# State-space inputs: three chunks' step-size products move into the pipeline, with their copy on VectorE and the softplus at the end

## The reference

```python
xz = x @ in_proj_w.T
u, z = split(xz)                                   # 256 channels each
u = silu(causal_dwconv(u, conv_w, conv_b))         # 4 taps
x_dbl = u @ x_proj_w.T                             # 8 + 16 + 16 columns
dt, Bm, Cm = x_dbl[:8], x_dbl[8:24], x_dbl[24:]
delta = softplus(dt @ dt_proj_w.T + dt_proj_b)
y = selective_scan(u, delta, -exp(A_log), Bm, Cm) + u * D
y = y * silu(z)
return y @ out_proj_w.T
```

## Time and profile before

| what | value |
|---|---|
| runs | 2076.75, 2073.79, 2072.45 us (median 2073.79) |
| the profiled execution, its own time | 2079.87 us |
| its span in the trace | 2077.9 us |
| `mamba_inputs` of the first block | up to 62.64 us, where the scan's first instruction stands |
| `mamba_inputs` of the second block | 1192.11 to 1244.05 us |
| scans (64 scan instructions each) | 65.5 to 269.8 us and 1247.3 to 1451.4 us |
| mean granted clock of TensorE | 0.937 |

### The profile page before, as it was taken

The page is one execution under the profiler, slowest core; times in us unless marked ns, Lnnn a source line. Parts: engine busy times, 40 slices in busy tenths (PEclk is TensorE's granted clock), DMA queues, the critical chain, the costliest instruction groups (busy, mean ns, idle before and its releaser), DMA issues. The chain is left out here.

```text
span 2077.9 us, 46457 instructions
## 1 busy us (share of the span) xinstructions
PE 1798.5 (87%) x18012; PEld 902.7 (43%) x18012; DVE 1619.0 (78%) x3425; ACT 1117.0 (54%) x2083; POOL 542.9 (26%) x560
## 2 busy tenths in 40 slices
PE   6777788999799999997899977777768999999967
PEld 2222254444255555553444422222533555555534
DVE  5899965666788999984565559999658999998665
ACT  5544423222278888885322274443342888888815
POOL 2798930000200000001000029989230000000012
PEclk9899998999689999998799979999886999999969
DMA  5333300311312222211041004443012222222200
GB/s 174 117 122 120 123 11 0 82 51 31 102 30 49 53 53 57 53 27 26 3 87 51 26 20 133 124 121 102 1 43 77 49 54 57 56 61 44 34 8 21
DMA packets 64617, 127.37 MB, mean 61 GB/s; under 512 B 15959, under 2 KB 26741, under 8 KB 62925
## 3 DMA queue, kind: packets, MB, share of 16 engines
q1 hardware_dynamic: 64108, 123.88, 23.3%
q10 hardware_dynamic: 288, 0.52, 0.1%
HBM read 105.74 MB, written 17.43 MB: 59 GB/s over the span
## 5 line engine op out<-in xcount | busy, mean ns | idle before, releaser
L1644 ACT ACTIVATE a_probs<-a_ps_k 128x512 f32<-128x512 f32 (+3 forms) x1280 | 598.9, 545 | 229.6 <-PE a_ps_k L1556 129.8
L1538 PE MATMUL a_ps_q<-a_k_op,a_q_op 84*32 84x512 bf16 (+7 forms) x5120 | 536.5, 366 | 29.0 <-DVE a_maxes L1701 18.8
L1704 DVE TENSOR_REDUCE a_maxes<-a_ps_q 128x1 f32<-128x512 f32 x768 | 504.1, 686 | 65.9 <-PE a_ps_q L1538 63.2
L1552 PE MATMUL a_ps_k<-a_q_op,a_k_op 87*32 87x512 bf16 (+7 forms) x5120 | 518.9, 354 | 6.2 <-DMA a_q_op<-a_max_T 2.9
L1574 PE MATMUL a_ps_o<-a_probs,a_vh 128*32 128x512 f32 (+3 forms) x2752 | 318.7, 508 | 0.8 <-ACT a_probs L1644 0.8
L1538 PEld LDWEIGHTS a_ps_q<-a_k_op,a_q_op 72*32 72x32 bf16 (+1 forms) x5120 | 187.4, 97 | 175.2 <-DVE a_maxes L1704 68.7
L1701 DVE CUSTOM_DVE_ANT_0 a_ps_q<-a_ps_q,all_c_mask_q 128x128 f32<-128x128 f32 (+3 forms) x512 | 248.0, 496 | 7.6 <-PE a_ps_q L1538 6.4
L1552 PEld LDWEIGHTS a_ps_k<-a_q_op,a_k_op 75*32 75x32 bf16 (+1 forms) x5120 | 185.7, 96 | 141.7 <-ACT a_probs L1644 84.0
L979 ACT ACTIVATE e_silu<-e_psg,all_me_b 128x512 f32<-128x512 f32 x128 | 87.8, 687 | 227.9 <-PE e_psg L911 227.9
L1784 POOL CAST a_max_parts<-a_neg_max 128x16 bf16<-128x16 f32 x32 | 6.3, 197 | 756.1 <-DVE a_neg_max L1709 756.1
L1062 DVE SCALAR_TENSOR_TENSOR e_mid<-e_psv,all_me_b,e_silu 128x512 f32<-128x512 f32 x128 | 95.7, 749 | 129.3 <-PE e_psv L913 125.4
(11 more groups left out here) (265 smaller groups left out, 2396.9 us busy)
## 6 DMA issues: line engine op xcount, KB each, us to landing
m0sc_c_rows<-m_bc_rows SPq DMA_DIRECT2D x32, 512.0 KB, 3.6
e_w_rows<-e_comb SPq DMA_DIRECT2D x64, 256.0 KB, 3.2
m1sc_c_rows<-m_bc_rows SPq DMA_DIRECT2D x32, 512.0 KB, 3.6
a_outputs<-a_o_sb SPq DMA_DIRECT2D x512, 18.0 KB
a_q_op<-a_q_parts SPq DMA_DIRECT2D x30, 288.0 KB
a_k_op<-a_k_parts SPq DMA_DIRECT2D x30, 288.0 KB
m0sc_b_rows<-m_bc_rows SPq DMA_DIRECT2D x32, 256.0 KB
m1sc_b_rows<-m_bc_rows SPq DMA_DIRECT2D x32, 256.0 KB
```

The costliest lines, as they stand in the source:

```text
L1538: last = pe.matmul(ps_q[32 * r:32 * r + 32, use % QB, 0:width], q_op[h % SLOT][0:NR, part(t, r)], k_op[h % SLOT][0:NR, kc * CH:kc * CH + w ...
L1552: last = pe.matmul(ps_k[32 * r:32 * r + 32, b % KB, 0:width], k_op[h % SLOT][:, part(j, r)], q_op[h % SLOT][:, c * CH + first:c * CH + fir ...
L1644: act.activation(probs[:, n % PSLOT, 0:width], ps_k[:, b % KB, 0:width], ACT.Exp).then_inc(exp_done, 1)
L1704: dve.tensor_reduce(found, bank, AX.X, ALU.max).then_inc(q_read, 1)
```

## The change

The step-size products of chunks 0, 1 and 2 now follow the gate products of steps 2, 3 and 4; that of chunk 3 follows xd of chunk 3, as the last. VectorE copies those of chunks 0, 1 and 2 out of PSUM to `delta`, adding the bias, at the end of steps 2, 3 and 4, after the taps. ScalarE no longer has a softplus in the step loop. After the loop it takes the softplus of chunk 0 from SBUF in place (one instruction of 128x1024), the second part of chunk 3, the softplus of chunk 3 out of PSUM (two instructions, as before), and that of chunks 1 and 2 from SBUF. VectorE's last products are in the order 0, 3, 1, 2.

```diff
@@ mamba_inputs @@
+        dt_copied = m.sem("dt_copied")
@@ order of the products @@
-        for s in range(NC + 1):
+        for s in range(NC + 2):
             items += [("u", s, h) for h in range(NH2) if s < NC]
             items += [("xd", s - 2, 0)] if s >= 2 else []
-            items += [("gate", s - 1, h) for h in range(NH2) if s >= 1]
-        items += [("dt", c, h) for c in range(2) for h in range(NH2)]
-        items += [("xd", NC - 1, 0)]
-        items += [("dt", c, h) for c in range(2, NC) for h in range(NH2)]
-        reader = {"u": raw_copied, "xd": xd_ready, "dt": delta_ready, "gate": gate_ready}
+            items += [("gate", s - 1, h) for h in range(NH2) if 1 <= s <= NC]
+            items += [("dt", s - 2, h) for h in range(NH2) if s >= 2]
+        reader = {"u": raw_copied, "xd": xd_ready, "dt": dt_copied, "gate": gate_ready}
@@ ScalarE @@
             def softplus(c):
-                for h in range(NH2):
-                    act.wait_ge(made, product_made("dt", c, h))
-                    act.activation(delta[:, h, chunk(c)], bank("dt", c, h), ACT.Softplus,
-                                   bias=w["dt_b"][:, h:h + 1]).then_inc(delta_ready, 1)
+                act.wait_ge(dt_copied, NH2 * (c + 1))
+                act.activation(delta[:, :, chunk(c)], delta[:, :, chunk(c)], ACT.Softplus).then_inc(delta_ready, 1)
+
+            def last_softplus(h):
+                act.wait_ge(made, product_made("dt", NC - 1, h))
+                act.activation(delta[:, h, chunk(NC - 1)], bank("dt", NC - 1, h), ACT.Softplus,
+                               bias=w["dt_b"][:, h:h + 1]).then_inc(delta_ready, 1)
@@ ScalarE, step loop and tail @@
-                if s == NC + 1:
-                    softplus(0)
...
-            softplus(1)
+            softplus(0)
             second(NC - 1)
-            softplus(2)
-            softplus(3)
+            for h in range(NH2):
+                last_softplus(h)
+            for c in range(1, NC - 1):
+                softplus(c)
@@ VectorE, end of a step (after the taps) and tail @@
-            for c in range(NC):
-                dve.wait_ge(delta_ready, NH2 * (c + 1))
+                if 2 <= s <= NC:
+                    for h in range(NH2):
+                        dve.wait_ge(made, product_made("dt", s - 2, h))
+                        dve.tensor_scalar(delta[:, h, chunk(s - 2)], bank("dt", s - 2, h), w["dt_b"][:, h:h + 1], None,
+                                          ALU.add).then_inc(dt_copied, 1)
+            for n, c in ((1, 0), (3, NC - 1), (4, 1), (5, 2)):
+                dve.wait_ge(delta_ready, n)
                 dve.tensor_tensor(du[:, :, chunk(c)], delta[:, :, chunk(c)], u[:, :, chunk(c)], ALU.mult).then_inc(du_ready, 1)
```

## The result

The changed kernel takes 2090.74 us (median of 4, 2090.15 to 2095.76), the kernel before beside it 2075.27 (4 runs, 2072.45 to 2077.39): ratio 1.0063, 95% interval 1.0039 to 1.0087, so 8 to 18 us slower. The forecast had the direction, and its 6.2 us are about half of the size; its range, up to 2084.5, does not hold the time.

A forecast was written before the change was run, and what follows sets the result against it. No engine bounds the whole; the chain through the two inputs sections to the scan counts. First block +1.9, second +1.2, together +3.1, plus clock +3.1, is +6.2 us: 2073.79 gives 2080.0, range 2075.0 to 2084.5.

The forecast's parts named there:

- Steps 1 to 5: Inputs section up to the last xd: VectorE waits for step-size products; X +0.8 us in the first block, +1.1 second.
- X: When ScalarE reads xd of chunk 3; first block 54.33 us before, 55.1 forecast at full clock.
- Step 6: Tail from X to the scan: table load and softplus follow X; +1.1 us in the first block, +0.1 in the second.
- Step 7: TensorE's clock may fall ahead of u of chunk 3 and the last xd, each block; 0.75 to 0.8 us each, +3.1.
- Full clock at all four places: Rival: TensorE keeps full clock ahead of u of chunk 3 and the last xd; +3.1 us, 2076.9; chance 0.20.
- The wait costs nearly nothing: Rival: VectorE's wait is nearly free, with short taps and brief copies; 0 to +2 us, 2075; chance 0.09.
- Faster: Rival: four step-size products gone from ahead of the last xd, if chunk 3's taps end by about 49; 2068.7; chance 0.05.
- All four places low: Rival: lower clock at all four TensorE places, or taps disturbed as long as before; +9 to +11 us, 2084; chance 0.10.
- The table load: On ScalarE, taken as 1.28 us without a drain; the skill page's 1.38 us drain per switch would give 2082.8.

The follow-up runs named there:

- a_late: Changed kernel with VectorE's copies of the step-size products one step later; ratio 1.0010 to the kernel before.
- a_tail: Changed kernel with the softplus of chunk 0, and so the table load, back ahead of the last xd on ScalarE; ratio 1.0025 to the kernel before.
- c_late_tail: a_late with the softplus of chunk 0 ahead of the last xd and that of chunk 1 right behind it; ratio 0.9996 to the kernel before.
- a_again: The changed kernel run once more without an edit; ratio 1.0054 to the kernel before.
- b_pad: Kernel before with the step-size products widened from 8 to 128 rows by zeros; ratio 0.9984 to the kernel before.
- a_late_pad: Changed kernel with VectorE's copies one step later and step-size products zero-padded to 128 rows; ratio 0.9985 to the kernel before.
- a_late0: Changed kernel with only chunk 0's copies late, chunk 1's still ahead of the taps of chunk 3; ratio 1.0054 to the kernel before.
- b_rows: Kernel before with step-size products made from 128 rows of other data, real step sizes left out; ratio 0.9986 to the kernel before.
- c_best: a_late_pad with the softplus of chunk 0 ahead of the last xd and that of chunk 1 right behind it; ratio 0.9986 to the kernel before.
- a_rows: Changed kernel with step-size products made from 128 rows of other data, real step sizes left out; ratio 1.0038 to the kernel before.

## Why the prediction came out at half the size

**Steps 1 to 5 held.** The copies' order made VectorE wait, and the waits carried to X as worked out. Taking the excess of each low-clock product off the trace after shows it: 26.40, less 3.75 - 1.98 for u and 3.14 - 1.91 for xd of chunk 1, is 23.40 us in the first block; the forecast's X without the clock was 22.50 + 0.8 = 23.3. In the second it is 26.16 - 1.77 - 0.37 - 0.49 = 23.5 against 22.18 + 1.1 = 23.3. The taps of chunk 3 took 5.56 us (5.7 forecast), the copies 0.7 to 0.8 (0.69), the last xd at full clock 1.88.

The products that were not at full clock can be taken off in the other traces too. X then comes 21.0 us after the first xd in all four blocks of the kernel before, 23.4 to 23.6 in the four of the changed one, and 20.3 in both of a_late.

**Step 6 held:** 9.56 us for 9.45. a_tail and c_late_tail show that only part of it can be had back by moving the softplus: the cover that step 6 called unused had shrunk, which the prediction did not ask.

**Step 7 failed, in its size.** It put 0.75 to 0.8 us on each of two places in a block, at most 1.5 on each ("a little more for longer work"). In the first block the place ahead of u alone cost 1.77 + 1.23 = 3.0 us, in the second 2.1 and 0.5 more at the last xd; 5.6 us for both blocks where 3.1 stood, and 5.5 in a_again. Two errors made it. The bound of 1.5 came from one xd at the lower clock and was used for a longer chain of work: u, then xd of chunk 1, twice the work in a row. And I thought of the fall as a matter of luck at each place, though the first place was hit in both blocks of both traces of the changed kernel (distance from the first xd to the second 12.9 to 13.6 us each time, 10.6 to 10.8 without the excess).

The trace of the kernel before had shown the price of such a chain, in two rows that the prediction did not use. It is u of chunk 2 and xd of chunk 0, where no step-size product has run yet:

```profile
25.45 3.75 PE L293 MATMUL m0in_acc<-m0in_xT,all_m_in_T 128*128 128x512 f32 x4 [1.11 <-ACT m0in_xT L197]
29.13 2.66 PE L297 MATMUL m0in_acc<-m_u,all_m_x_T 128*40 128x512 f32 x4
```

Against 1.98 and 1.91 that is 2.5 us for one place, behind waits of 1.69 and 1.11 us that are no longer than those which rows 2 show at full clock.

With 5.6 in place of 3.1 the sum is 8.7 us, and the traces show 8.1 to 9.3. The rest to the measured ratio is not located, and is within its interval. Step 7 alone does not explain that the time lies outside the range: 2073.79 + 8.7 is 2082.5, still inside. The measured 2090.74 is 10.7 above the forecast's 2080.0, of which 2.5 are step 7 and 1.5 the median of the kernel before (2075.27 with a fourth run, not 2073.79). Most of the rest stands between the executions of the kernel before: the traced one took 2079.87, 6 above the median that the forecast was added to, and the changed kernel's traced one 2090.15, by 10.3 more. In later runs the medians of the kernel before were 2079.5 to 2083.3. What makes its executions differ so is open.

**The rivals.** "Full clock at all four places" is out, with the rule that was set beside it: rows 7 showed a busy TensorE losing its clock, and b_pad shows that 128 rows, zeros included, hold it. "The wait costs nearly nothing" is out. "Faster" had half of its condition: a_late takes VectorE's waits away, and the taps of chunk 3 end at 47.1 in its first block, but X then came about where the kernel before has it, or 1.0 us before b_pad's if the clock holds (a_late_pad), and not 3.3 us earlier. The four products gone from ahead of the last xd are six in the changed order, those of chunks 0 to 2, and TensorE has to make them all first. "All four places low" was nearest to the time, by its total and not by its mechanism: three places of four were hit, the two ahead of u for 3.0 and 2.1 us, one ahead of the last xd for 0.5.

**The table load.** In the trace after, as before, 1.28 us and the next instruction 0.01 behind it; nothing like the drain that the Trainium skill sets beside it (ScalarE: Activation LUTs, What ACT_TABLE_LOAD costs).

## What to carry to other kernels

An instruction that waits for a product must not stand ahead of work that the product's own engine needs next: VectorE's copy waited for TensorE while TensorE's next transposes waited behind the copy. Put a copy that nobody needs soon one step late. Before a stage is reordered, look at where the clock fell in the trace and behind what; work in the lower clock's reach is a term to be summed over its whole chain, with the rows' own lengths at either level. Where narrow products stand ahead of a critical chain, padding their rows with zeros cost no time on TensorE here and kept its clock; when it pays must be measured.

## What the runs showed of the hardware

- Products of 8 rows let TensorE's clock fall to 1.2 GHz though the engine is busy all through: behind four of them in all four blocks traced of the kernel before (0.54 in the first). Behind two of them, four transposes and a wait of 0.78 us it fell in five of six blocks (a_late, where it was low for 6.8 us in the first block, a_late0 and c_late_tail). Widened to 128 rows, with data or with zeros, they take the same time and the clock stays at 1.00 behind them: in four of four blocks at the first place (b_rows, b_pad) and four of four at the second (a_late_pad, c_best). "TensorE: Matmul & The Clock Gate" (The Trainium skill, section "What's actually happening") has the clock follow how busy the engine has been; here the number of rows counts too.
- A wait of TensorE can bring a fall as well (a_rows, low for 3.4 us), and wait and narrow products together gave the longer one (6.8 us in the changed kernel). How long a fall lasts varied from run to run: u of chunk 3 and xd of chunk 1 took 3.75 and 3.10 us in the first block of a_late, 3.36 and 1.91 in that of a_late0, and 1.96 and 1.91 in the second of c_late_tail.
